# A second set of row buffers and an earlier place for the last stream stores in a mixture-of-experts decoder layer

## The reference, cut to what matters

```python
x = x + linear_attention(layernorm(x))            # 8 x 256 tokens, 512 wide, 16 heads
x = x + long_convolution(ctx, layernorm(x))       # 32 heads of 8
h = layernorm(x).reshape(2048, 512)
w, sel = route(h)                                 # 4 of 16 experts for each token
out = sum over e: w_e * (silu(h @ g_e.T) * (h @ u_e.T)) @ d_e.T       # experts, hidden width 256
shared = (silu(h @ sg.T) * (h @ su.T)) @ sd.T
return x + out + shared
```

## Time and profile before

| | |
|---|---|
| median of 3 runs | 906.6 us (906.11 to 910.64) |
| profiled execution, its own time | 913.62 us |
| its span, first to last instruction | 911.5 us |
| mean granted TensorE clock | 0.988 |
| busy | PE 858.1 us (94%), DVE 574.7 us (63%), ACT 376.9 us (41%), POOL 376.9 us (41%) |
| part of the kernel that the change touches | about 515 to 600 us of the span |
| routed slots | from 530 us to the end, one after the other |

### The profile page before, as it was taken

The page is one execution under the profiler, slowest core; times in us unless marked ns, Lnnn a source line. Parts: engine busy times, 40 slices in busy tenths (PEclk is TensorE's granted clock), DMA queues, the critical chain, the costliest instruction groups (busy, mean ns, idle before and its releaser), DMA issues.

```text
span 911.5 us, 14031 instructions
## 1 busy us (share of the span) xinstructions
PE 858.1 (94%) x4369; PEld 705.8 (77%) x4369; DVE 574.7 (63%) x888; ACT 376.9 (41%) x607; POOL 376.9 (41%) x383
## 2 busy tenths in 40 slices
PE   5999999999899999899999989799999999999994
PEld 5888888888777777668787778677777877877784
DVE  5666666656469999999769855344445443454431
ACT  5312322233134433332652245355555555645552
POOL 0300000001136685551622324656666666656644
PEclk9999999999999999999999999899999999999998
DMA  8500000000027533330210366887888888888856
GB/s 293 182 1 0 1 0 0 0 0 12 10 61 210 161 115 93 116 104 18 83 59 6 133 240 194 165 199 188 209 184 200 198 191 204 184 199 201 192 110 88
DMA packets 50946, 109.45 MB, mean 120 GB/s; under 512 B 8864, under 2 KB 11424, under 8 KB 50784
## 3 DMA queue, kind: packets, MB, share of 16 engines
q0 software_dynamic: 17024, 40.48, 23.6%
q1 hardware_dynamic: 33888, 68.55, 23.3%
HBM read 78.35 MB, written 30.65 MB: 120 GB/s over the span
## 4 chain that ended last, share of the span: by engine, by line
PE 63%; DVE 18%; issue 10%; ACT 3%; DMA 2%; POOL 1%; DVEq 0%; POOLq 0%; ACTq 0%; SPq 0%
PE PS L196 16%; PE PS L198 16%; PE PS L197 16%; PE PS L207 6%; DVE QY L916 5%; PE PS L1481 2%; DVE term L910 2%; PE PS L535 2%; PE PS L597 2%; DVE QY_rounded L1732 1%; DVE term L900 1%; ACT hTh L1276 1%; DVE wl L1727 1%; DMA out_y<-QY,idy 1%; DMA out_y<-X 1%
## 5 line engine op out<-in xcount | busy, mean ns | idle before, releaser
L196 PE MATMUL PS<-QY_rounded,wh 128*128 128x512 f32 (+1 forms) x376 | 153.8, 409 | 2.0 <-DVE QY_rounded L1732 1.3
L198 PE MATMUL PS<-QY_rounded,wl 128*128 128x512 f32 (+1 forms) x376 | 146.7, 390 | 0.0
L1205 POOL DMA_INDIRECT out_y<-QY,idy x72 | 118.1, 1640 | 43.9 <-ACT QY L1295 27.4
L197 PE MATMUL PS<-QY_rounded,wh 128*128 128x512 f32 (+1 forms) x312 | 120.1, 385 | 0.0
L1745 DVE TENSOR_TENSOR hTl<-hh,hTh 128x512 fp32r<-128x512 f32 (+1 forms) x39 | 26.5, 679 | 124.9 <-ACT hTh L1276 120.9
L1187 POOL DMA_INDIRECT xg<-xs_d,idx x72 | 84.9, 1179 | 32.3 <-issue 15.8
L207 PE MATMUL PS<-qER,Tz 128*128 128x288 f32 x320 | 81.4, 409 | 8.7 <-DVE low_rounded L757 5.5
L264 POOL TENSOR_SCALAR var_eps<-mean_var 128x2 f32<-128x2 f32 x15 | 4.1, 270 | 196.7 <-DVE mean_var L379 196.7
L198 PEld LDWEIGHTS PS<-QY_rounded,wl 128*128 128x128 f32 x376 | 71.0, 189 | 15.3
L196 PEld LDWEIGHTS PS<-QY_rounded,wh 128*128 128x128 f32 x376 | 71.6, 191 | 13.9 <-issue 1.5
L207 PE MATMUL PS<-prod,Tz 128*128 128x288 f32 x320 | 81.4, 410 | 0.1
(11 more groups left out here) (215 smaller groups left out, 1849.4 us busy)
## 6 DMA issues: line engine op xcount, KB each, us to landing
ws<-in_gu_w SPq DMA_DIRECT2D x38, 512.0 KB
ws<-in_dn_w SPq DMA_DIRECT2D x20, 512.0 KB, 5.6
C<-in_ctx SPq DMA_DIRECT2D x32, 256.0 KB, 2.6
Tz<-kpad_d SPq DMA_DIRECT2D x32, 256.0 KB, 3.2
xs_d<-xn SPq DMA_DIRECT2D x16, 256.0 KB, 2.0
out_y<-X SPq DMA_DIRECT2D x16, 256.0 KB
X<-in_x SPq DMA_DIRECT2D x1, 3072.0 KB, 18.0
xg<-xs_d,idx POOLq DMA_INDIRECT x72
```

Source lines behind the costliest of these rows:

```text
L196: pe.matmul(out_, lh, rh, start=first, stop=False)
L197: pe.matmul(out_, lh, rl, start=False, stop=False)
L198: return pe.matmul(out_, ll, rh, start=False, stop=last)
L1205: nc.gpsimd.indirect_dma_start(out=out, out_offset=bass.IndirectOffsetOnAxis(ap=idy[:, t:t + 1], axis=0), in_=yo[:, t], in_offset=None, co ...
```

## The change

- The second slot's rows go into two buffers of their own (`second`), laid over `prod0` and `xn3`, with semaphores `second_in`. Its gathers are issued right behind those of the first slot, without a wait. The third slot's gathers go out, without the small copy of their indices, when the first slot's transposes are done. The copy of slot 1's weights becomes two copies.
- The last shared group's down passes for tiles 1, 2 and 3 stand behind the first slot's transposes 1, 2 and 3, and ACT's copies of them likewise. DVE adds the whole group right behind `add_shared(2)`, ahead of the first slot's hidden values.
- SP stores all four groups of the stream ahead of the last weight part of slot 1.

```diff
+        second = [flat[:, 0:2 * (D + NE)].rearrange("p (t n) -> p t n", t=2) for flat in
+                  (prod[0][:].rearrange("p c b n -> p (c b n)"), xn3_all[:].rearrange("p k n -> p (k n)"))]
+        second_in = [sem(f"second{t}_in") for t in range(SLOT_T)]
+        def is_second(s):
+            return isinstance(s, int) and s == 1
+        def rows_of(s, t):
+            return second[t // 2][:, t % 2] if is_second(s) else xg[:, t]
+        def rows_in(s, t):
+            if is_second(s):
+                return second_in[t], 16
+            return xg_in[t], 16 if isinstance(s, int) and s == 0 else 16 * s
...
-                for g in range(NG - 1):
+                for g in range(NG):
                     store_group(g)
                 next_part(e, 0, 2)
                 e = expert_of(sp, 2)
-                next_part(e, 1, 0)
-                next_part(e, 1, 1)
-                store_group(NG - 1)
-                next_part(e, 1, 2)
+                for part in range(NPART):
+                    next_part(e, 1, part)
...
-                def gathers(s, first=False):
-                    if not first:
-                        wait_apart(pool, xT_ps5, DC * s)
-                        wait_apart(pool, wpos_done, s)
+                def gathers(s):
+                    fixed = isinstance(s, int) and s < 3
+                    if not fixed or s == 2:
+                        wait_apart(pool, xT_ps5, DC if fixed else DC * s)
+                        wait_apart(pool, wpos_done, 1 if fixed else s)
+                    if not fixed:
                         nc.gpsimd.tensor_copy(idx[:], IDX[:, bass.ds(SLOT_T * s, SLOT_T)]).then_inc(idx_done, 1)
-                        wait_apart(pool, idx_done, s)
+                        wait_apart(pool, idx_done, s - 2)
...
-                gathers(0, first=True)
+                gathers(0)
+                gathers(1)
                 more = more_slots(pool)
                 last = more + (NFULL - 1)
                 weights(0)
-                gathers(1)
+                gathers(2)
                 weights(1)
-                gathers(2)
                 wait_apart(pool, x3_out, 16 * NT)
                 scatters(0, first=True)
...
                 def next_parts(s, final=False):
-                    if isinstance(s, int) and s == 0:
-                        y_shared_out(NG - 1, 2)
-                        y_shared_out(NG - 1, 3)
...
                 x_hi(0, 2)
+                y_shared_out(3, 2)
                 x_hi(0, 3)
+                y_shared_out(3, 3)
...
                             slot_gate_up(s, 1, d)
-                            if first and d == 0:
-                                down5(NG - 1, 2)
-                                down5(NG - 1, 3)
                             x_transposed(s + 1, d)
...
                     x_transposed(0, d)
-                    if d == 1:
-                        down5(3, 1)
+                    if d > 0:
+                        down5(3, d)
...
-                    if isinstance(s, int) and s == 1:
-                        add_shared(NG - 1)
...
                 add_shared(2)
+                add_shared(3)
```

More of the change, by code:

```diff
@@ L1184, in gathers @@
                         nc.gpsimd.tensor_copy(idx[:], IDX[:, bass.ds(SLOT_T * s, SLOT_T)]).then_inc(idx_done, 1)
-                        wait_apart(pool, idx_done, s)
+                        wait_apart(pool, idx_done, s - 2)
                     for t in range(SLOT_T):
-                        nc.gpsimd.indirect_dma_start(out=xg[:, t], out_offset=None, in_=xs_d,
-                                                     in_offset=bass.IndirectOffsetOnAxis(ap=(IDX if first else idx)[:, t:t + 1], axis=0)
-                                                     ).then_inc(xg_in[t], 16)
+                        at_ = IDX[:, SLOT_T * s + t:SLOT_T * s + t + 1] if fixed else idx[:, t:t + 1]
@@ L1191, in weights @@
+                        nc.gpsimd.indirect_dma_start(out=rows_of(s, t), out_offset=None, in_=xs_d,
+                                                     in_offset=bass.IndirectOffsetOnAxis(ap=at_, axis=0)
+                                                     ).then_inc(rows_in(s, t)[0], 16)
                 def weights(s):
                     for t in range(SLOT_T):
-                        wait_apart(pool, xg_in[t], 16 * (s + 1))
+                        wait_apart(pool, *rows_in(s, t))
                     e = expert_of(pool, s)
-                    nc.gpsimd.tensor_copy(WPOS[:, bass.ds(SLOT_T * s, SLOT_T)].unsqueeze(2), xg[:, :, bass.ds(e + D, 1)]
-                                          ).then_inc(wpos_done, 1)
+                    if is_second(s):
+                        nc.gpsimd.tensor_copy(WPOS[:, SLOT_T:SLOT_T + 2].unsqueeze(2), second[0][:, :, bass.ds(e + D, 1)])
+                        nc.gpsimd.tensor_copy(WPOS[:, SLOT_T + 2:2 * SLOT_T].unsqueeze(2), second[1][:, :, bass.ds(e + D, 1)]
+                                              ).then_inc(wpos_done, 1)
+                    else:
+                        nc.gpsimd.tensor_copy(WPOS[:, bass.ds(SLOT_T * s, SLOT_T)].unsqueeze(2), xg[:, :, bass.ds(e + D, 1)]
+                                              ).then_inc(wpos_done, 1)
@@ L1479, in x_transposed @@
                         if d == 0:
-                            pe.wait_ge(xg_in[t], 16 * (s + 1))
-                        mm = pe.transpose(PS[:, 4 + d % 2, t * P:(t + 1) * P], xg[:, t, d * P:(d + 1) * P], ident[:])
+                            pe.wait_ge(*rows_in(s, t))
+                        mm = pe.transpose(PS[:, 4 + d % 2, t * P:(t + 1) * P], rows_of(s, t)[:, d * P:(d + 1) * P], ident[:])
                     mm.then_inc(xT_ps5, 1)
```

## The result

| | kernel before | changed kernel |
|---|---|---|
| median of 20 runs | 909.75 us (906.11 to 913.91) | 903.6 us (902.32 to 906.5) |
| profiled execution | 913.62 us, span 911.5 | 903.55 us, span 901.4 |

The ratio is 0.994, 95% interval 0.9926 to 0.9953: faster by 0.6%, 5.5 us by the ratio and 6.2 by the medians. Forecast were -8.2 us and 898.4, with 895.5 to 903.5 as the range for 8 in 10; 903.6 lies just above it. The two profiled executions are 10.1 us apart, more than forecast; the runs are not.

The account below looks back on a forecast made before the run. TensorE's own stream was taken as the bound, except for a slot 2 stall waiting for `y_out` behind late stores and scatters. Terms -7.5 - 0.7 = -8.2 us; 906.6 - 8.2 = 898.4 us, 8-in-10 range 895.5 to 903.5.

Parts of the forecast that it names:

- the main term: Last four stream stores issued directly behind the twelve others; the slot 2 stall goes entirely, -7.5 us.
- The stall of 7.53 us: Slot 2 to 3 takes 26.44 us instead of 18.91: 4.89 us wait for `y_out`, 2.4 us low clock.
- The first rival: The stall is smaller without the profiler; only 1.2 us to be had, 905.4, no measurable change; chance 0.12.
- Scatters at silu plus 3.0: Sign of being right: the first scatter starts 3 us after its slot's silu, no longer held by stores.
- No clock dip from 570 to 593: Sign of being right: the granted clock no longer dips in the slices from 570 to 593 us.
- these gathers: Second and third slot's gathers issued earlier; their rows' waits were hidden behind the low-part chain, priced at 0.
- The landing of 8.58 us: Time from issue to landing of the first slot's last scatter, used to find 3.6 us to spare.
- The estimate of 2.6 us: Landing of a 256 KB scatter by the Trainium skill's GpSimd DMA price; would leave 9.6 us to spare, same sum.
- The moved down passes: 12 matmuls moved before slot 0 fill idle time; slot 0's chain ends earlier, -0.4 to -1.7, taken as -0.7 us.
- the bound that I called less likely: Before slot 0, the register load hides fully behind queued matmuls; slot starts at 532.4, giving -1.7 us.
- The first gathers late: Rival: second gathers run beside the first and delay PE's transposes up to 2.4 us; -5.8 in all, 900.8; chance 0.08.
- The low clock in slot 0: Rival: two close pauses drop TensorE to 1.2 GHz for a slot, 14.5 us, giving 912.9; chance 0.04.

Follow-up runs that it names:

- experiment 6: Changed kernel, next slot's first column block split ahead of its first weight part: slot 0 alone 902.89 us, ratio 0.9943; all slots 894.78 us, 0.9846.
- buffers alone: Kernel before with only the second slot's own row buffers and the earlier gathers: 908.03 us, ratio 0.9985.
- experiment 5: Changed kernel with slot 1's gathers issued behind the first weight copy instead of directly behind the first gathers: 904.93 us, ratio 0.9942.
- stores alone: Kernel before with down passes, their copies, additions and stores moved, but one row buffer as before: 907.28 us, ratio 0.9964.
- sixth profile: Kernel before, unchanged, profiled a sixth time: execution of 911.14 us, PE waiting 3.4 us for `y_out`.
- held-back variant: Kernel before, SP issuing slot s+1's second weight part only after the scatters of slot s-2 have landed: 908.37 us, ratio 0.9987.
- 907.54 us trace: Kernel before, unchanged, timed and profiled once more: 910.99 us, ratio 1.0009; its profiled execution took 907.54 us.

## Why the prediction was right or wrong

**Where it failed.** The step is the last one of the sum, the main term and what it was taken from: "So the whole 7.53 us go" and "Against the median, 906.6 - 8.2". The stall of 7.53 us was read from one profiled execution of 913.6 us and taken off the median of runs. Six profiles of the kernel before give 97.7 to 102.7 us from the indices to slot 4, on average 100.5; the changed kernel has 94.0 both times. The gain is 3.7 to 8.7 us, on average 6.5, as the medians say (6.2). Slot 0 gives 1.1 of it, so the main term, forecast at 7.5, is 2.6 to 7.7 by trace and 5.4 on average. The median of three runs was also 3.15 us under that of twenty, which by itself moves 898.4 to 901.6; the other 2.0 us up to 903.6 are what the term was too large by (7.5 - 5.4).

The first rival had seen the 7.0 us between profile and median but asked whether they come from the profiler. They don't: without a profile, executions of up to 913.9 us occur. Of the 20 runs 9 are at 906.1 to 908.4 and 11 at 909.6 to 913.9, and the three known ones, 910.6, 906.6 and 906.1, had this spread already. Not all of it is the stall: the indices themselves come at 514.1 to 515.6 us in the six traces, and the changed kernel, which has no stall, spreads over 4.2 us.

**The stores, point by point.** The stall's place and its chain were right, and so was the gain against the one execution that had it in full: 7.5 us in slot 2. The last store was expected to be issued at 541.3 to 543.3 and came at 539.7; landed by 551.4 at worst, it was 546.4. Scatters at silu plus 3.0, it was 2.98. No clock dip from 570 to 593: right. That it is the place of the stores which does this was too narrow: with the old place, 3.2 of 5.5 us stay. The earlier gathers take 1.08 MB out of the stores' way, which then land 2.7 to 2.8 us sooner; these gathers were priced at 0.

**The landing of 8.58 us** was taken as a constant. It is 5.5 to 8.6 in the kernel before, and most of the difference goes with a 512 KB weight part issued beside the scatter. The Trainium skill's rule that DMAs of different issuers share 16 engines and interleave (DMA: Bandwidth & Descriptors, "Issuing engines are not separate DMA queues") agrees with these landings, and it belonged to this step. The estimate of 2.6 us, which the prediction made by that page's fit, agrees with none of them.

**The moved down passes.** -0.4 to -1.7 forecast, -0.7 taken, -1.1 measured: slot 1's silu moves from 38.5 to 37.4 behind the indices. The gap before slot 0 closed entirely, the bound that I called less likely: the first slot matmul follows the last shared one at 532.20 without idle time, and the register load now began at 529.3, ahead of the last transposes. For a closed gap the forecast was -1.7; the missing 0.6 is mostly PE's wait of 0.72 us ahead of it (next point). PE then waits 1.0 us for the low part, and experiment 6 shows that this chain was the limit, as the prediction said.

**The first gathers late.** In part: ACT's first high part is 1.8 instead of 0.7 us behind the transposes, and PE waits 0.7 us for the low part, where 2.4 were priced. With the buffers alone, without the passes between, that price is paid, with the low clock in it: slot 0's silu comes 2.7 us later. Whether the 0.7 us reach the end is not shown; experiment 5 took the cause away and gained nothing.

**The low clock in slot 0**, the rival on the other side, didn't come in the changed kernel: 1.00 from 527 to 570 us, with pauses of 0.7 and 1.0 us. With the stores alone and with the buffers alone the traces have it, for some 3 us each, behind waits for rows or their low parts.

What decides whether slot 2's rows are in time is not found; issue times of the gathers and stores ahead of them agree within 0.1 us in both sorts (0.2 in the sixth profile).

## What to carry to other kernels

Before a stall from one trace is taken off a median, compare the trace's own time with the spread of the runs; if the times spread by as much as the stall, take several traces, see whether the stall goes with the time, and forecast its mean. A wait that ends in a DMA landing is priced with what else is issued in that microsecond, and moving one transfer out of the way may be worth as much as moving the one that is waited for. When the long stall is gone, the small wait that every slot has is the larger sum: here 0.5 us in each, by swapping two operations.

## What the runs showed of the hardware that was not expected

- The last scatter of the first slot, 256 KB, landed in 5.5 to 6.2 us when no 512 KB load was issued for 1.7 us or more behind its issue, and in 8.3 to 8.6 us when one was issued within 0.1 us of the end of its issue (kernel before and held-back variant).
- After PE's wait of 3.4 to 5.0 us the granted clock fell in each of four traces (0.94 three times and 0.89 over 570 to 600 us), and also after 2.5 us (0.94). After one wait of 2.0 us (907.54 us trace) it stayed at 1.00. But three waits of 1.0, 0.7 and 1.0 us one after the other were followed by 0.71 from 542 to 546 us (stores alone), and in the trace with idle times of 1.5 and 0.5 us the clock was 0.74 and 0.83 from 530 to 538 us (buffers alone). The longest wait alone doesn't tell.
- PE's register load of the slot count takes 1.4 to 1.7 us in the six traces of the kernel before, and PE then idles 1.2 to 1.5 us behind eight short transposes. Behind six matmuls of 512 columns there is no idle time, also with a load of 1.56 us (experiment 5). That the load is what PE waits for is read from the times; the profile names a DVE operation.
